# A fused adaLN transformer block: normalising a batch on two engines, Pool's rows ahead of its routing, and three small units half a step later

## The chip, the cores and the metric

The kernel runs on one core of a Trainium2 chip. The metric is the device time in microseconds of one execution: 648.39 us is the median of three (647.23 to 651.87). The core's engines run side by side, each through its own queue in program order, and wait for one another on semaphores: TensorE (PE in the rows, PEld for its weight loads), VectorE (DVE), ScalarE (ACT), GpSimd (POOL), and SyncE (SP), which here only issues DMAs.

## The reference

Eight sequences of 512 tokens with 128 features go through multi-query attention with 16 heads of 8 (one K and V for all heads), then a mixture of experts with 8 experts and top 2, each behind a modulated layer norm.

```python
mod = (_silu(L0_c) @ L0_wmod).reshape(L0_c.shape[0], 6, 1, -1)
h = _layernorm(x) * (1 + ca) + sa
x = x + ga * attention(h)            # softmax(q k^T / sqrt(8)) v, 16 heads, one k and v
h = _layernorm(x) * (1 + cb) + sb
logits = einsum('bth,eh->bte', h, router_w)          # 8 experts, the best 2 taken
h1 = gelu(einsum('bth,efh->btef', h, w1) + b1)
expert_outputs = einsum('btef,ehf->bteh', h1, w2) + b2
x = x + gb * sum(topk_expert_outputs * softmax(topk_values))
```

## The kernel before

**Three stages.** A preparation (to about 65 us) normalises, projects and stores Q, K and V. The attention loop (about 65 to 452 us) does the attention and, beside it, the second layer norm, the router and the routing of the rows. The expert stage (to the end) runs 71 tiles of 128 routed rows.

**The attention loop.** It has 32 groups g: group g does four heads (g mod 4) of batch g // 4. A group has four steps s (128 keys or queries each), a step has four quarter steps j, and two of these are a half step u, for which ScalarE computes one exponential of 128x1024 (L1270). Per half step TensorE issues two quartets of row maxima for the group after next (`maximum(g + 2, s, j)`, L1055), two quartets of scores (`scores`, L1088) and, mostly, two quartets of values (`values`, L1099). VectorE reduces each row-maximum result out of PSUM (L1408). The rows' maxima are turned (L1074), copied by ScalarE (L1295), split in three by GpSimd (L76 to L79) and written by SyncE into the Q operand of the next group, so that the scores come out with the maximum taken off.

**What limits how far TensorE runs ahead.** The maxima and some small units ("maxima turned", "heads turned", "rows turned", "logits", "ranks") share a ring of three PSUM banks: a unit waits until the unit three places before it is reduced by VectorE or copied by ScalarE. `ring_order` lists the units, and TensorE's loop must issue them in the same order. `scores` of a half step waits for the exponential two half steps before it.

**The side work.** For batch b, `batch_at(g, n)` says that group g is 4(b + 1) + n. Counting groups by their number mod 4:

- group 1 mod 4: heads turned (n = 1) and copied by ScalarE (`heads_out`, L1305), ranks of an earlier batch (n = 5; `ranks_out`, L1319); GpSimd does `slots` and `add_attention` (L695 to L699).
- group 2 mod 4: VectorE does four `stats` (L1424) in step 1; GpSimd does `route(b, 0)` and then the variance and a Newton root.
- group 3 mod 4 (n = 3): ScalarE normalises four columns of tokens (`normalize_rows`, L1280), two after the exponential (s, u) = (0, 1), two after (1, 0). GpSimd scales and shifts them (`rows`, L738 to L742). It also does `route` of another batch, pieces 1 and 2. TensorE turns the rows at (s, j) = (3, 3) (L1133).
- group 0 mod 4: logits (n = 4; L1141, copied at L1313); GpSimd does `route(b, 3)` and `top_two`.

`rows` runs in the loop for batches 0 to 5 (groups 7, 11, 15, 19, 23, 27), `route` pieces 1 and 2 in the same place for batches 0 to 4 (groups 11, 15, 19, 23, 27). One `route(b, t)` is two indirect DMAs (L810), each of 128 rows of 576 bytes to places in HBM that the core computed. GpSimd starts them itself. Its order in a group is: split of the next group's maxima, then slots, add_attention, route 0, variance and root, route 1, rows, route 2, route 3, top_two, as far as the group has them.

## Time and profile before

| | us |
|---|---|
| median of the runs | 648.39 |
| the profiled execution | 644.04 |
| its span, first to last instruction | 642.2 |
| PE busy | 568.3 |
| DVE busy | 500.9 |
| ACT busy | 446.0 |
| POOL busy | 318.3 |

The profiled execution is 0.7% under the median. Busy time is a union over the engine's instructions, and for matmuls the ends are modelled, so a busy PE is not a PE without stalls. In rows of a timeline the start of an instruction is what to trust. In the attention loop TensorE shows the same repeating pattern of quartets, so its stalls are read from the distance of two starts.

### The profile page before, as it was taken

To read this page: it belongs to the slowest core of one execution; us is meant where nothing else is said; L and a number is where in the kernel's file an instruction comes from. 1 tells how busy PE (TensorE), PEld (TensorE's weight loads), DVE (VectorE), ACT (ScalarE), POOL (GpSimd) and SP (SyncE) were. 2 spreads that over 40 slices of the span, in tenths; PEclk is the share of its full clock that TensorE was granted. 3 is DMA by queue.
4 is the path that set the end of the run, shared out by engine and by line. 5 is a ranking of instruction groups with operands and counts; after the bars stand their busy time and mean duration, and the time that the engine had idled before them with its cause. 6 is when DMAs were issued, how large, how long until landed. Compare 5 with 4: busy or idle time off the path is not lost.

```text
span 642.2 us, 21095 instructions
## 1 busy us (share of the span) xinstructions
PE 568.3 (88%) x7723; PEld 345.8 (54%) x7723; DVE 500.9 (78%) x1134; ACT 446.0 (69%) x776; POOL 318.3 (50%) x574
## 2 busy tenths in 40 slices
PE   3779999999999999999999999989888897898980
PEld 2222444454544554554454554543777887798970
DVE  5778999898888888888888888786656475555697
ACT  5683688788878878879778878778634452447671
POOL 2633110143476666666566666653166446454571
PEclk9889999999999999999999999999999898799995
DMA  6298300300300310310310310001232122232645
GB/s 182 75 304 301 109 12 8 89 20 8 96 20 26 102 24 26 98 28 22 100 26 26 91 36 24 26 25 30 61 94 67 50 73 85 64 90 59 195 138 169
DMA packets 49877, 49.46 MB, mean 77 GB/s; under 512 B 15616, under 2 KB 44336, under 8 KB 49056
## 3 DMA queue, kind: packets, MB, share of 16 engines
q1 hardware_dynamic: 42256, 36.89, 20.4%
q0 software_dynamic: 4320, 9.38, 4.5%
q10 hardware_dynamic: 3200, 1.84, 1.0%
q8 instruction: 64, 1.05, 0.7%
q14 instruction: 37, 0.30, 0.2%
HBM read 29.40 MB, written 17.10 MB: 72 GB/s over the span
## 4 chain that ended last, share of the span: by engine, by line
PE 66%; DVE 8%; ACT 6%; issue 5%; SPq 4%; another core or an unknown queue 3%; DMA 3%; POOL 1%; DVEq 0%; POOLq 0%; ACTq 0%
PE ps L1055 15%; PE ps L1088 14%; PE ps L1099 13%; PE ps L1178 8%; PE ps L1167 8%; DVE neg_max L1408 3%; ACT P L1270 2%; SPq L956 2%; DMA Q<-max_parts 2%; PE ps L1126 1%; PE ps L1141 1%; SPq L946 1%; PE ps L1158 1%; PE ps L1074 1%
## 5 line engine op out<-in xcount | busy, mean ns | idle before, releaser
L1408 DVE TENSOR_REDUCE neg_max<-ps 128x1 f32<-128x512 f32 x512 | 325.2, 685 | 52.6 <-PE ps L1055 49.6
L1270 ACT ACTIVATE P<-ps,zero 128x1024 f32<-128x1024 f32 x256 | 279.4, 1117 | 71.8 <-PE ps L1088 67.7
L1055 PE MATMUL ps<-K,Q 128*32 128x512 bf16 x2048 | 194.2, 383 | 6.1 <-DVE neg_max L1408 5.0
L1088 PE MATMUL ps<-Q,K 128*32 128x512 bf16 x2048 | 157.1, 381 | 10.7 <-ACT P L1270 4.3
L1099 PE MATMUL ps<-P,V 128*32 128x256 f32 x2048 | 157.7, 382 | 0.5 <-ACT P L1270 0.5
L1620 POOL DMA_INDIRECT y_rows<-P,to_now x71 | 71.3, 1004 | 87.1 <-DVE P L1460 47.5
L1326 ACT ACTIVATE parts<-ps,parts 128x128 f32<-128x128 f32 x228 | 63.8, 382 | 59.1 <-PE ps L1167 27.0
L1055 PEld LDWEIGHTS ps<-K,Q 128*32 128x32 bf16 x2048 | 54.7, 96 | 77.6 <-DVE neg_max L1408 32.0
L1088 PEld LDWEIGHTS ps<-Q,K 128*32 128x32 bf16 x2048 | 52.7, 97 | 69.5 <-ACT P L1270 14.1
L1099 PEld LDWEIGHTS ps<-P,V 128*32 128x32 f32 x2048 | 61.6, 110 | 48.3 <-issue 2.9
L810 POOL DMA_INDIRECT h_sorted<-diag,slot x64 | 64.3, 1004 | 28.6 <-POOL max_parts L79 13.4
L1167 PE MATMUL ps<-parts 128*128 128x128 f32 x456 | 64.8, 282 | 8.6 <-issue 5.8
L1178 PE MATMUL ps<-W,parts 128*128 x456 | 63.1, 283 | 2.6 <-ACT parts L1326 1.5
L1167 PEld LDWEIGHTS ps<-parts 128*128 128x128 f32 x456 | 57.5, 195 | 11.6 <-issue 9.5
L1178 PEld LDWEIGHTS ps<-W,parts 128*128 128x128 f32 x456 | 57.6, 198 | 3.9 <-issue 3.8
L76 POOL CAST max_parts<-neg_max_T 16x128 bf16<-16x128 f32 x32 | 9.0, 281 | 100.0 <-ACT neg_max_T L1295 100.0
L1441 DVE COPY parts<-W 128x644 f32 x57 | 29.8, 523 | 19.3 <-issue 10.3
L1460 DVE TENSOR_TENSOR P<-ps,parts 128x128 f32<-128x128 f32 x57 | 16.3, 285 | 26.7 <-PE ps L1178 14.0
L1326 ACT ACTIVATE P<-ps,P 128x128 f32<-128x128 f32 x56 | 16.0, 371 | 17.2 <-remote 6.7
L1158 PE MATMUL ps<-consts,xs 128*128 128x128 f32 x71 | 19.7, 282 | 0.2 <-issue 0.2
L1448 DVE COPY parts<-ps 128x128 f32<-128x128 f32 x57 | 16.2, 284 | 3.6 <-PE ps L1158 2.8
L1262 ACT COPY att_u<-ps 128x512 f32<-128x512 f32 x32 | 18.5, 577 | 0.8 <-PE ps L1099 0.8
(239 smaller groups left out, 584.3 us busy)
## 6 DMA issues: line engine op xcount, KB each, us to landing
Q<-q_parts SPq DMA_DIRECT2D x24, 384.0 KB
xs<-h_sorted SPq DMA_DIRECT2D x71, 72.0 KB
W<-w_t SPq DMA_DIRECT2D x2, 2048.0 KB, 11.1
q_parts<-parts SPq DMA_DIRECT2D x8, 384.0 KB, 4.0
Q<-y_rows SPq DMA_DIRECT2D x6, 512.0 KB
diag<-att_u SPq DMA_DIRECT2D x128, 16.0 KB
Q<-max_parts SPq DMA_DIRECT2D x96, 4.0 KB
out<-Q SPq DMA_DIRECT2D x6, 256.0 KB, 2.3
```

The lines of the kernel that those rows point to most:

```text
L810: eng.indirect_dma_start(h_sorted, bass.IndirectOffsetOnAxis(ap=slot[p][:, k, t:t + 1], axis=0), hs[p][:, t, :], None).then_inc(routed[p], 16)
L1055: ins = eng.matmul(ring_bank(*unit)[QUAD * q:QUAD * (q + 1), :], Q[buffer_of(g)][:, g % NG * G + j, at:at + QUAD], K[buffer_of(g)][:, 0, : ...
L1088: ins = eng.matmul(to, K[p][:, 1, at:at + QUAD], Q[p][:, first:first + 2, some], start=True, stop=True, tile_position=(0, QUAD * q))
L1099: ins = eng.matmul(bank(7)[QUAD * j:QUAD * (j + 1), some], V[buffer_of(g)][:, s, :], P[s % 2][:, j, some], start=(s == 0 and u == 0), stop ...
L1158: eng.transpose(bank(TURN_BANK[t % 2])[:, 0:TS], xs[t % XD][:, 0:D], ident).then_inc(xsT_done, 1)
L1167: ins = eng.matmul(bank(t % UD)[:, TS * c:TS * (c + 1)], w1_now[t % HD][:, 128 * c:128 * (c + 1)], xsT[t % HD], start=True, stop=True)
L1178: ins = eng.matmul(bank(DOWN_BANK[t % 2])[:, 0:D], hid[t % HD][:, c, :], W2[:, bass.ds(e, 1), c, :].rearrange("p a d -> p (a d)"), start=( ...
L1270: nc.scalar.activation(P[s % 2][:, :, HALF * u:HALF * (u + 1)], bank(2 * u, 2).rearrange("p (j t) -> p j t", j=G), ACT.Exp, bias=zero[:], ...
L1326: nc.scalar.activation(hid[t % HD][:, c, :], bank(t % UD)[:, TS * c:TS * (c + 1)], ACT.Gelu, bias=w1_now[t % HD][:, F + c:F + c + 1]).then ...
L1408: eng.tensor_reduce(neg_max[g % 2][:, j * T + s:j * T + s + 1], ring_bank("maximum", g, s, j), AX.X, ALU.max, negate=True).then_inc(ring_u ...
L1441: eng.tensor_copy(w1_now[t % HD], W1[:, bass.ds(e, 1), :].rearrange("p a d -> p (a d)")).then_inc(w_copied, 1)
L1620: eng.indirect_dma_start(y_rows, bass.IndirectOffsetOnAxis(ap=to_now[t % YD], axis=0), ys[t % YD], None).then_inc(scattered[t % YD], 16)
```

## The change

Four things change.

1. ScalarE normalises only columns 0 and 2 of the batch: column 0 after the exponential (0, 1), column 2 after (1, 1).
2. VectorE normalises columns 1 and 3, each as one `tensor_scalar`: column 1 after the reduction of quarter step (0, 3), column 3 after that of (1, 3). `normalized`, which did this for one late batch only, now takes a list of columns.
3. In GpSimd's queue, `rows` stands ahead of `route(…, 1)`, no longer behind it.
4. Heads, logits and ranks are issued by TensorE at quarter step (2, 1) instead of (1, 3), and copied by ScalarE ahead of the exponential (2, 1) instead of (2, 0). The ring's order follows.

```diff
-                        if s == 1 and j == 3 and batch_at(g, 1) is not None:
+                        if s == 2 and j == 1 and batch_at(g, 1) is not None:
                             units.append(("heads turned", batch_at(g, 1)))
...
-                        if s == 1 and j == 3 and batch_at(g, 4) is not None:
+                        if s == 2 and j == 1 and batch_at(g, 4) is not None:
                             units.append(("logits", batch_at(g, 4)))
-                        if s == 1 and j == 3 and batch_at(g, 5) is not None:
+                        if s == 2 and j == 1 and batch_at(g, 5) is not None:
                             units.append(("ranks", batch_at(g, 5)))
...
-                            if s == 2 and u == 0 and batch_at(g, 1) is not None:
+                            if s == 2 and u == 1 and batch_at(g, 1) is not None:
                                 heads_out(batch_at(g, 1))
...
-                            if s == 0 and u == 1 and batch_at(g, 3) in IN_LOOP:
-                                normalize_rows(batch_at(g, 3), (0, 1))
-                            if s == 1 and u == 0 and batch_at(g, 3) in IN_LOOP:
-                                normalize_rows(batch_at(g, 3), (2, 3))
+                            if s < 2 and u == 1 and batch_at(g, 3) in IN_LOOP:
+                                normalize_row(batch_at(g, 3), 2 * s)
...
-                def normalized(b):
+                def normalized(b, these=range(T)):
...
-                    for n in range(b * T, (b + 1) * T):
+                    for n in (b * T + t for t in these):
                         eng.tensor_scalar(xn2[b % 2][:, n - b * T, :], X[:, n, :], rstd2[:, n:n + 1], shift2[:, n:n + 1],
                                           ALU.mult, ALU.add).then_inc(xn2_done, 1)
...
+                            if s < 2 and j == 3 and batch_at(g, 3) in IN_LOOP:
+                                normalized(batch_at(g, 3), (2 * s + 1,))
...
+                    if batch_at(g, 3) in IN_LOOP:
+                        rows(eng, batch_at(g, 3))
                     if batch_at(g, 7) in EARLY:
                         route(eng, batch_at(g, 7), 1)
-                    if batch_at(g, 3) in IN_LOOP:
-                        rows(eng, batch_at(g, 3))
                     if batch_at(g, 7) in EARLY:
                         route(eng, batch_at(g, 7), 2)
```

GpSimd's queue in a group 3 mod 4 (from group 11 on), before. L79 ends the split of the maxima, each L810 is one indirect DMA of a route, L738 to L742 are `rows`, and L76 begins the split of the next group.

```order
L79 TENSOR_TENSOR max_parts<-max_rest,max_parts 16x128
L810 DMA h_sorted<-diag,slot 34816x144 x2
L738 COPY diag<-consts 128x4
L740 TENSOR_TENSOR diag<-diag,mod_row 128x512
L742 TENSOR_TENSOR diag<-diag,mod_row 128x4x128
L810 DMA h_sorted<-diag,slot 34816x144 x2
L76 CAST max_parts<-neg_max_T 16x128
```

The same place of the changed kernel:

```order
L79 TENSOR_TENSOR max_parts<-max_rest,max_parts 16x128
L738 COPY diag<-consts 128x4
L740 TENSOR_TENSOR diag<-diag,mod_row 128x512
L742 TENSOR_TENSOR diag<-diag,mod_row 128x4x128
L810 DMA h_sorted<-diag,slot 34816x144 x4
L76 CAST max_parts<-neg_max_T 16x128
```

The two pairs of indirect DMAs, which had the two long instructions of `rows` between them, stand together as four in a row.

ScalarE's queue in the same group, before: L1262 copies the finished values of the group before out of PSUM, L1270 is an exponential, L1280 a normalised column, L1309 the copy of the turned rows.

```order
L1295 COPY neg_max_T<-ps 16x128
L1270 ACTIVATE P<-ps,zero 128x4x256
L1262 COPY att_u<-ps 128x512
L1280 ACTIVATE diag<-X,shift,rstd 128x128 x2
L1270 ACTIVATE P<-ps,zero 128x4x256
L1280 ACTIVATE diag<-X,shift,rstd 128x128 x2
L1270 ACTIVATE P<-ps,zero 128x4x256 x5
L1309 COPY diag<-ps 128x512
```

And of the changed kernel (its lines are one to four lower from here on; L1279 is the normalisation):

```order
L1294 COPY neg_max_T<-ps 16x128
L1270 ACTIVATE P<-ps,zero 128x4x256
L1262 COPY att_u<-ps 128x512
L1279 ACTIVATE diag<-X,shift,rstd 128x128
L1270 ACTIVATE P<-ps,zero 128x4x256 x2
L1279 ACTIVATE diag<-X,shift,rstd 128x128
L1270 ACTIVATE P<-ps,zero 128x4x256 x4
L1308 COPY diag<-ps 128x512
```

Two of four columns are gone from ScalarE, and two exponentials stand between the two that are left.

## Rows read from the trace of the kernel before

**Rows 1.** The page: span, and busy time of each engine with its share.

```profile
span 642.2 us, 21095 instructions
...
PE 568.3 (88%) x7723; PEld 345.8 (54%) x7723; DVE 500.9 (78%) x1134; ACT 446.0 (69%) x776; POOL 318.3 (50%) x574
```

**Rows 2.** Windows: us; busy PE, PEld, DVE, ACT, POOL; PE clock; DMA share, GB/s.

```profile
184.00:232.00 48.00, 46.77 (x787) 23.19 (x783) 40.31 (x68) 38.88 (x49) 30.73 (x66) 1.00 0.19 51
...
432.60:435.80 3.20, 3.20 (x32) 1.32 (x36) 2.86 (x10) 2.45 (x3) 1.73 (x5) 0.52 0.03 6
```

**Rows 3.** Groups by shape: count, busy us, mean ns of one, idle before.

```profile
L1408 DVE TENSOR_REDUCE neg_max<-ps 128x1 f32<-128x512 f32 x512 | 325.2, 685 | 52.6 <-PE ps L1055 49.6 <-PE ps L1133 1.4
...
L1431 DVE TENSOR_SCALAR diag<-X,rstd,shift 128x128 f32<-128x128 f32 x8 | 2.2, 342 | 1.9 <-POOL shift L729 1.9
```

**Rows 4.** Timeline of ACT, groups 7 and 8: start, us, instruction, idle before.

```profile
149.67 0.58 ACT L1262 COPY att_u<-ps 128x512 f32<-128x512 f32 x1
150.14 0.89 ACT L1280 ACTIVATE diag<-X,shift,rstd 128x128 f32<-128x128 f32 x2
150.92 1.11 ACT L1270 ACTIVATE P<-ps,zero 128x1024 f32<-128x1024 f32 x1
...
161.81 0.58 ACT L1262 COPY att_u<-ps 128x512 f32<-128x512 f32 x1
```

**Rows 5.** Timeline of PE, group 7; x4 is one quartet, x8 two.

```profile
151.18 0.60 PE L1099 MATMUL ps<-P,V 128*32 128x256 f32 x8
151.61 0.39 PE L1055 MATMUL ps<-K,Q 128*32 128x512 bf16 x4
152.08 0.62 PE L1088 MATMUL ps<-Q,K 128*32 128x512 bf16 x8
...
153.17 0.39 PE L1055 MATMUL ps<-K,Q 128*32 128x512 bf16 x4
153.84 0.40 PE L1088 MATMUL ps<-Q,K 128*32 128x512 bf16 x4 [0.28 <-ACT P L1270]
```

**Rows 6.** Timeline of ACT, groups 15 and 16: the same copy in both.

```profile
246.55 0.58 ACT L1262 COPY att_u<-ps 128x512 f32<-128x512 f32 x1
...
259.36 0.58 ACT L1262 COPY att_u<-ps 128x512 f32<-128x512 f32 x1
```

**Rows 7.** Timeline of POOL, group 15.

```profile
248.09 1.09 POOL L810 DMA_INDIRECT h_sorted<-diag,slot  x1 [0.83 <-POOL max_parts L79]
...
252.09 1.29 POOL L742 TENSOR_TENSOR diag<-diag,mod_row 128x512 f32<-128x512 f32 x1
253.67 1.03 POOL L810 DMA_INDIRECT h_sorted<-diag,slot  x1 [0.28 <-POOL diag L742]
255.00 0.97 POOL L810 DMA_INDIRECT h_sorted<-diag,slot  x1 [0.30 <-issue]
```

**Rows 8.** Timeline of DVE, group 15: the longest wait for a maximum.

```profile
250.42 0.69 DVE L1408 TENSOR_REDUCE neg_max<-ps 128x1 f32<-128x512 f32 x1 [1.44 <-PE ps L1055]
```

**Rows 9.** Timeline of POOL, groups 29 and 30: first and last of four starts.

```profile
425.53 1.08 POOL L810 DMA_INDIRECT h_sorted<-diag,slot  x1 [0.81 <-POOL slot L803]
...
429.44 1.02 POOL L810 DMA_INDIRECT h_sorted<-diag,slot  x1 [0.30 <-issue]
```

**Rows 10.** Timeline of PE, group 30: the scores and the waits before them.

```profile
426.45 0.61 PE L1088 MATMUL ps<-Q,K 128*32 128x512 bf16 x8
...
427.81 0.62 PE L1088 MATMUL ps<-Q,K 128*32 128x512 bf16 x8
...
430.30 0.61 PE L1088 MATMUL ps<-Q,K 128*32 128x512 bf16 x8 [1.39 <-ACT P L1270]
432.60 1.04 PE L1088 MATMUL ps<-Q,K 128*32 128x512 bf16 x8 [1.69 <-ACT P L1270]
```

**Rows 11.** Timeline of ACT, group 30: the exponentials of those two scores.

```profile
429.13 1.11 ACT L1270 ACTIVATE P<-ps,zero 128x1024 f32<-128x1024 f32 x1 [1.82 <-PE ps L1088]
...
431.44 1.10 ACT L1270 ACTIVATE P<-ps,zero 128x1024 f32<-128x1024 f32 x1
```

**Rows 12.** Timeline of POOL and DVE: end of group 13, first stats of 14.

```profile
232.03 1.28 POOL L699 TENSOR_TENSOR X<-X,gated 128x512 f32<-128x512 f32 x1
...
235.13 0.28 DVE L1424 BATCH_NORM_STATS2 ln_stats<-X 128x6 f32<-128x128 f32 x1
```

More of the change, by code:

```diff
@@ L1201, in _ @@
                                 scores(g, s, j // 2)
-                            if s == 1 and j == 3 and batch_at(g, 1) is not None:
+                            if s == 2 and j == 1 and batch_at(g, 1) is not None:
                                 turn_heads(batch_at(g, 1))
@@ L1209, in _ @@
                                 logits(LAST - 1)
-                            if s == 1 and j == 3 and batch_at(g, 4) is not None:
+                            if s == 2 and j == 1 and batch_at(g, 4) is not None:
                                 logits(batch_at(g, 4))
-                            if s == 1 and j == 3 and batch_at(g, 5) is not None:
+                            if s == 2 and j == 1 and batch_at(g, 5) is not None:
                                 ranks(batch_at(g, 5))
@@ L1271, in exponentials, with normalize_row @@
                                          ACT.Exp, bias=zero[:], scale=SCALE).then_inc(exp_done, 1)
-                def normalize_rows(b, tokens):
+                def normalize_row(b, t):
                     eng.wait_ge(rstd2_own, START + (b + 1) * NEWTON_OPS)
@@ L1277, in normalize_rows @@
                         eng.wait_ge(rows_own, START + (b - 1) * ROWS_OPS)
-                    for t in tokens:
-                        n = b * T + t
-                        nc.scalar.activation(xn2[b % 2][:, t, :], X[:, n, :], ACT.Identity, bias=shift2[:, n:n + 1],
-                                             scale=rstd2[:, n:n + 1]).then_inc(xn2_done, 1)
+                    n = b * T + t
+                    nc.scalar.activation(xn2[b % 2][:, t, :], X[:, n, :], ACT.Identity, bias=shift2[:, n:n + 1],
+                                         scale=rstd2[:, n:n + 1]).then_inc(xn2_done, 1)
                 def copy_sums(b, turned):
@@ L1352, in _ @@
                                 turned(batch_at(g, 4))
-                            if s == 2 and u == 0 and batch_at(g, 4) is not None:
+                            if s == 2 and u == 1 and batch_at(g, 4) is not None:
                                 logits_out(batch_at(g, 4))
-                            if s == 2 and u == 0 and batch_at(g, 5) is not None:
+                            if s == 2 and u == 1 and batch_at(g, 5) is not None:
                                 ranks_out(batch_at(g, 5))
@@ L1424, in stats @@
                     eng.bn_stats(ln_stats[:, b * T + t, :], X[:, b * T + t, :]).then_inc(stat_own, 1)
-                def normalized(b):
+                def normalized(b, these=range(T)):
                     eng.wait_ge(rstd2_own, START + (b + 1) * NEWTON_OPS)
-                    eng.wait_ge(rows_own, START + (b - 1) * ROWS_OPS)
-                    for n in range(b * T, (b + 1) * T):
+                    if b >= 2:
+                        eng.wait_ge(rows_own, START + (b - 1) * ROWS_OPS)
+                    for n in (b * T + t for t in these):
                         eng.tensor_scalar(xn2[b % 2][:, n - b * T, :], X[:, n, :], rstd2[:, n:n + 1], shift2[:, n:n + 1],
```

## The prediction

> **What bounds the kernel now.** I read the page first, then windows over the attention loop, then the timelines of PE, ACT, DVE and POOL side by side in the groups that the change touches. The page has TensorE busy for 568.3 of 642.2 us [rows 1]; over four groups of the loop it is 46.77 of 48.00 us, at full clock [rows 2]. TensorE's time is what a change must shorten or lengthen here. Busy is modelled, so I count stalls by starts: two quartets take 151.61 - 151.18 = 0.43 us [rows 5], one 0.215, and whatever two starts lie further apart than that is lost. VectorE is close behind: a reduction is written down with 685 ns [rows 3] and TensorE needs about 0.65 us per maximum.
>
> Group 7 is the one with the normalisation but without routing. From its copy L1262 to the next group's it takes 161.81 - 149.67 = 12.14 us [rows 4]. TensorE loses there 152.08 - 151.61 - 0.215 = 0.25 and 153.84 - 153.17 - 0.215 = 0.45 us, both before scores, the second with ScalarE's exponential as the releaser [rows 5]. So the group would be 11.44 us without stalls. Group 15, with routing, takes 259.36 - 246.55 = 12.81 [rows 6]: 1.37 us of stalls, 0.70 of them like those of group 7 and 0.67 more.
>
> What those 0.67 us are is the centre of this prediction. GpSimd starts an indirect DMA at 248.09 and three more by 255.00 [rows 7]. VectorE, with nothing else to do, gets a maximum from TensorE only at 250.42, after 1.44 us of idleness [rows 8]. The finer case is in groups 29 and 30, the only place where four starts stand together, 425.53 to 429.44 + 1.02 = 430.46 [rows 9]. Scores begun at 426.45 on TensorE reach ScalarE at 429.13, 2.68 us later; those begun at 427.81 at 431.44, 3.63 us later and 0.98 us after the last start's end [rows 10, 11]. Two quartets need 0.43 us of that. So while GpSimd is inside an indirect DMA, word of TensorE's finished work arrives late. I don't know why; the trace shows that it is so. TensorE itself runs on until it needs an answer, and then stands: 430.30 - 427.81 - 0.86 = 1.63 us (two quartets of scores, two of values lie between), and 432.60 - 430.30 - 0.43 = 1.87 us [rows 10], 3.5 us in all.
>
> **The change part by part.**
>
> *ScalarE's two columns less.* Two columns are 0.78 us from start to start (150.92 - 150.14) [rows 4]. Before, ScalarE had an extra 0.47 + 0.78 + 0.78 = 2.03 us within two exponentials (150.14 - 149.67 is the 0.47). An exponential starts every 1.02 us when ScalarE is behind and TensorE asks for one every 1.29 (six quartets), a slack of 0.27. Afterwards it is 0.47 + 0.39 after (0, 1), nothing after (1, 0), 0.39 after (1, 1); by my count of the starts every exponential ends before the scores that need it. I take the whole 0.70 us: **6 groups x 0.70 = -4.2 us**. The least it can be is nothing, if what is left still delays.
>
> *VectorE's two columns more.* 342 ns recorded each [rows 3], about 0.26 in its queue. Twice per group, three and a half quarter steps apart at least, against a ring that lets VectorE be about 0.8 us late before TensorE notices. I take 0. If the cover were gone it would be 6 x 2 x 0.26 = 3.1 us. Here a rule of the Trainium skill bears (SBUF — State Buffer, Who interferes with whom): a `tensor_scalar` may use the port pair that VectorE shares with GpSimd, and whoever comes second is blocked for the other's whole instruction. By it the first column could wait for one of GpSimd's short splits, and the sum would be up to 2 us higher. No row here shows the normalisation beside a busy GpSimd. The second column cannot meet `rows`, which waits for it.
>
> *Rows ahead of routes.* `rows` now starts when the last column is there. In group 11's or 15's times that is about 1 us after `rows` began before; the two long instructions take 1.3 us each (252.09 + 1.29 is the end of the second) [rows 7], so `rows` is done earlier than before and TensorE's turning at (3, 3) does not wait. What is late next are the routes: all four starts come behind, in one run of 1.33 + 3 x 1.27 = 5 us (429.44 + 1.02 - 425.53 = 4.93) [rows 9]. They begin about one step before the group's end and cover the beginning of the next group, where the first exponential, the copy of the turned maxima and VectorE's reductions all wait for TensorE.
>
> The cost of one run of four is bounded from both sides. Below: it costs what the pairs cost now, 0.67 us, so nothing more. Above: the 3.5 us of group 30. I walk it through: counted from the first start, the scores of the next group's first half step begin at about +2.2. Judging by group 30 they are seen at +5.7 to +5.9 (431.44 - 425.53), the exponential ends at +6.9, and only then can TensorE issue the scores two half steps on, due at +4.5: 2.4 us lost, and half a microsecond more because the copy of the turned maxima, which frees a ring bank, stands behind that exponential. I take **2.9 us**, nearer to group 30 because the mechanism is the same and only the work around differs (here the turned rows give TensorE 0.7 us that need no answer, there the maxima are at their end). Against 0.67 now that is +2.2 us for each of the five groups 11, 15, 19, 23, 27: **+11.2 us**.
>
> *Heads, logits, ranks half a step later.* The same work in the same ring distances. In group 1 mod 4 TensorE has no stall to give back; I take 0. GpSimd's work behind the ranks comes about 1.3 us later: `add_attention` ended at 232.03 + 1.28 = 233.31, now at about 234.6. VectorE's first of four stats waits for it; it stood at 235.13, so 0.5 us of slack are left [rows 12]. If that is gone, six groups pay up to 0.8 us each, 5 us. In group 0 mod 4 the later logits may save some tenths of a stall: 0 to -1 us in all, taken as 0.
>
> **The sum.** -4.2 + 11.2 = +7.0 us. On the profiled execution that is 644.04 + 7.0 = 651; the median stands 4.35 us above that execution, so I say 648.39 + 7.0 = 655.4, rounded 655.5.
>
> **The rivals.**
>
> *A. Four starts cost no more than two pairs.* Then ScalarE's gain stands alone: 648.39 - 4.2 = 644.2, with the logits' share 643. This is the case on the other side. It decides at a cost per run of four of 0.67 + 4.2/5 = 1.5 us: below that the kernel is not slower. For it speaks that a pair costs only 0.67; against it that late news does not add up evenly: the first microsecond and a half fall into TensorE's slack and only the rest is lost, so a run twice as long costs more than twice as much. A rule of the Trainium skill is on this rival's side (SBUF — State Buffer, SBUF: two separate sides): PE and ACT never wait on anyone at SBUF's ports, and a DMA cannot be slowed by compute nor slow it. By it four starts would cost TensorE nothing by position. The late results of group 30 don't contradict a rule on ports, but they show that something else is late. Chance 0.3.
>
> *B. The clock falls too.* After the two waits of group 30 the granted clock was 0.52 over the next 3.20 us [rows 2]: TensorE did the work of 1.6 us in that time, a loss of 1.5. If the stall in all five groups is followed by this, add 7.5 us: 663. For it: the waits are alike. Against: between my two waits TensorE does more work than there. Chance 0.15.
>
> *C. The stats wait.* `add_attention` is late for the stats by more than its slack: up to 5 us on top, 660. Chance 0.05.
>
> The forecast itself, a run of four costing 1.5 to 3.7 us, has 0.5 and by itself gives 648.4 to 659.
>
> **How the numbers follow.** The range reaches from A's time, 644, to 664 where B and the upper bound end. Since cases of both signs hold most of the chance, the forecast's own range is 650 to 659. A measurement of this kernel can tell about 1%, 6.5 us, from no change. Faster by over 1% needs 641.9 or less, more than all of ScalarE's gain: 0.05. Slower by over 1% is 654.9 or more: B, C and about half of the forecast's case: 0.47. Within 1%: A and the lower half of the forecast, 0.48.
>
> **What would show each step.** Group 7, which has no routing, should shrink from 12.14 to about 11.45 us between its copies L1262, with no start of scores late; if it doesn't, the first term is wrong. Groups 11 to 27 (every fourth) should grow from 12.8 to about 14.4 us, part of it seen in the group behind, with four starts of L810 about 1.3 us apart, an exponential at the next group's head that waits 2 us or more for PE L1088, and PE starts over 1 us late just behind. If these groups get shorter, A is right. A clock below 1.00 behind these places shows B. The first stats of a group 2 mod 4 with GpSimd as releaser shows C. The groups 1 mod 4 should stay at their time. Most likely to be wrong is the size of a run of four, since one place in the trace has to speak for five.

## The result, and the profile after

| | before | after |
|---|---|---|
| median of 20 executions | 648.94 us (645.02 to 651.96) | 655.89 us (649.9 to 663.81) |
| ratio after / before | | 1.0083, 95% interval 1.0062 to 1.0104 |
| the profiled execution | 644.04 us | 656.22 us |

The changed kernel is 0.8% slower. Three of the 20 executions of after (661.47, 663.81 and 661.15 us) are in a slow state, and the ratio leaves them out while the medians count them. The ratio stands for 5.4 us (4.0 to 6.7), the two medians lie 6.95 us apart, and the two profiled executions 12.2 us. The last of these overstates the change: the profile of before is an execution quicker than all 20 timed ones, that of after an ordinary one. Sums over the two traces are read with that in mind; single places are not touched by it.

The page of after. It answers [rows 1] and, with the reduction L1405, [rows 3] (685 ns, 52.6 us idle):

```profile
span 654.3 us, 21103 instructions
...
PE 568.0 (87%) x7723; PEld 348.5 (53%) x7723; DVE 505.7 (77%) x1146; ACT 442.1 (68%) x764; POOL 318.1 (49%) x574
...
L1405 DVE TENSOR_REDUCE neg_max<-ps 128x1 f32<-128x512 f32 x512 | 328.3, 686 | 58.3 <-PE ps L1055 47.8
...
L1055 PE MATMUL ps<-K,Q 128*32 128x512 bf16 x2048 | 197.0, 386 | 19.2 <-DVE neg_max L1405 17.1
```

TensorE's work is unchanged (568.3 and 568.0 us), ScalarE has 4 us less and VectorE 5 us more. What grew is TensorE's idle time, above all before maxima that wait for VectorE: 19.2 us, where the page of before has 6.1.

**Where it went.** As in the prediction, a group is measured from its copy L1262 to the next one. The groups whose length changed by more than 0.15 us behind the first one:

| groups | before | after | change |
|---|---|---|---|
| 7 (columns, no routing) | 12.14 | 11.41 | -0.73 |
| 11 + 12 | 25.39 | 28.75 | +3.36 |
| 15 + 16 | 25.11 | 26.58 | +1.47 |
| 19 + 20 | 25.79 | 27.24 | +1.45 |
| 23 + 24 | 24.96 | 27.99 | +3.03 |
| 27 + 28 | 25.29 | 26.99 | +1.70 |
| 10, 14, 18, 22, 26 together | 58.89 | 60.38 | +1.49 |
| 25 | 11.77 | 12.30 | +0.53 |
| 29 + 30 + 31 | 33.99 | 34.77 | +0.78 |

The attention loop, from the first copy to the last, went from 371.67 to 384.84 us, +13.2; the expert stage behind it takes the same (189.96 and 189.56).

**A run of four starts, in after.** GpSimd in group 11 (timeline: start, us, instruction, idle before):

```profile
202.89 1.10 POOL L810 DMA_INDIRECT h_sorted<-diag,slot  x1 [0.29 <-POOL diag L742]
204.29 0.97 POOL L810 DMA_INDIRECT h_sorted<-diag,slot  x1 [0.30 <-issue]
205.56 0.96 POOL L810 DMA_INDIRECT h_sorted<-diag,slot  x1 [0.30 <-issue]
206.83 0.95 POOL L810 DMA_INDIRECT h_sorted<-diag,slot  x1 [0.30 <-issue]
```

TensorE, ScalarE and VectorE over it (`remote` means that the profile names no engine of this core as what ended the wait):

```profile
204.27 0.40 PE L1055 MATMUL ps<-K,Q 128*32 128x512 bf16 x4
204.48 0.61 PE L1088 MATMUL ps<-Q,K 128*32 128x512 bf16 x8
204.91 0.40 PE L1055 MATMUL ps<-K,Q 128*32 128x512 bf16 x4
...
205.68 0.28 PE L1074 MATMUL ps<-consts,neg_max 128*16 128x128 f32 x1
206.50 0.40 PE L1055 MATMUL ps<-K,Q 128*32 128x512 bf16 x4 [0.54 <-DVE neg_max L1405]
206.72 0.60 PE L1088 MATMUL ps<-Q,K 128*32 128x512 bf16 x8
209.45 0.62 PE L1055 MATMUL ps<-K,Q 128*32 128x512 bf16 x4 [2.12 <-DVE neg_max L1405]
209.85 1.07 PE L1099 MATMUL ps<-P,V 128*32 128x256 f32 x8
```
```profile
207.31 1.11 ACT L1270 ACTIVATE P<-ps,zero 128x1024 f32<-128x1024 f32 x1 [2.53 <-remote]
208.83 0.26 ACT L1294 COPY neg_max_T<-ps 16x128 f32<-16x128 f32 x1 [0.40 <-remote]
```
```profile
205.75 0.69 DVE L1405 TENSOR_REDUCE neg_max<-ps 128x1 f32<-128x512 f32 x1 [1.71 <-PE ps L1055]
208.70 2.11 DVE L1405 TENSOR_REDUCE neg_max<-ps 128x1 f32<-128x512 f32 x3 [2.26 <-remote]
```

Scores begun at 204.48 reach ScalarE at 207.31, 2.83 us later, much as in [rows 10, 11]. The maximum begun at 204.27 reaches VectorE at 205.75, 1.48 us later, and the one begun at 204.91 only at 208.70, 3.79 us later and behind the last start (206.83 + 0.95 = 207.78). These two free the ring banks that TensorE needs next: the maxima of 206.50 and 209.45 each start 0.06 us after the end of the reduction of the unit three places before (205.75 + 0.69 = 206.44, and the first of the three from 208.70 on, 209.39). TensorE stands 206.50 - 205.68 - 0.21 = 0.61 and 209.45 - 206.72 - 0.43 = 2.30 us: **2.9 us together**. Both waits end with VectorE's reduction. The exponential from 207.31 on was over at 208.42, about 1 us before TensorE went on. The rows can't tell whether the matmuls end late or only the word of it is late, since their ends are modelled.

The other four runs of four in groups 15 to 27 look the same: 0.5 to 0.6 us of standing, then 2.3 us in three of them and 1.6 us in the fourth (group 23). A sixth run of four, from 438.59 to 443.09 + 0.96 = 444.05 in groups 29 and 30, costs far less: group 30 lasts 11.04 us, against 10.63 us where no result is late (run e5 below).

**The clock behind it.** Windows of 3 us behind the five runs of four (columns as in [rows 2]):

```profile
209.80:212.80 3.00, 3.00 (x36) 1.19 (x32) 1.69 (x4) 1.43 (x3) 1.84 (x4) 0.52 0.19 44
262.50:265.50 3.00, 3.00 (x64) 1.53 (x60) 2.99 (x6) 2.70 (x4) 1.84 (x4) 1.00 0.18 49
313.00:316.00 3.00, 3.00 (x60) 1.54 (x56) 2.99 (x6) 2.70 (x4) 1.84 (x4) 1.00 0.20 44
363.40:366.40 3.00, 3.00 (x36) 1.20 (x32) 1.89 (x4) 2.13 (x3) 1.39 (x4) 0.52 0.16 30
416.30:419.30 3.00, 3.00 (x64) 1.53 (x60) 2.99 (x6) 2.70 (x4) 1.84 (x4) 1.00 0.05 11
```

Behind two of five the granted clock was about half, 1.2 instead of 2.4 GHz, and TensorE issued 36 instead of 60 to 64 instructions. These are the groups that lost 3.36 and 3.03 us; the other three lost 1.5 to 1.7.

**The late stretch.** Before TensorE turns the last rows (L1133) there is a wait that before did not have; it ends with VectorE's L742:

```profile
451.28 0.61 PE L1088 MATMUL ps<-Q,K 128*32 128x512 bf16 x8
454.67 0.80 PE L1133 MATMUL ps<-consts,diag 128*128 128x128 f32 x4 [2.77 <-DVE diag L742]
```

### The profile page after: what moved, and what is told of

The parts are those of the page before. It is cut to its first block, busy times and chain, and to the rows that moved or that the text cites. A ratio compares the mean times of both kernels' runs of the same rounds, so it can differ in the third digit from the quotient of the medians.

```text
span 654.3 us, 21103 instructions
## 1 busy us (share of the span) xinstructions
PE 568.0 (87%) x7723; PEld 348.5 (53%) x7723; DVE 505.7 (77%) x1146; ACT 442.1 (68%) x764; POOL 318.1 (49%) x574
## 4 chain that ended last, share of the span: by engine, by line
PE 63%; DVE 8%; SPq 6%; DMA 5%; another core or an unknown queue 5%; issue 4%; POOL 3%; ACT 3%; DVEq 0%; POOLq 0%; ACTq 0%
PE ps L1055 16%; PE ps L1088 13%; PE ps L1099 13%; PE ps L1167 7%; PE ps L1178 7%; DVE neg_max L1405 3%; SPq L956 3%; DMA Q<-max_parts 3%; DMA k_parts<-parts 1%; PE ps L1126 1%; SPq L946 1%; PE ps L1141 1%; POOL h_sorted L810 1%; ACT parts L1325 1%
## 5 line engine op out<-in xcount | busy, mean ns | idle before, releaser
L1405 DVE TENSOR_REDUCE neg_max<-ps 128x1 f32<-128x512 f32 x512 | 328.3, 686 | 58.3 <-PE ps L1055 47.8
L1270 ACT ACTIVATE P<-ps,zero 128x1024 f32<-128x1024 f32 x256 | 279.9, 1116 | 86.6 <-PE ps L1088 64.4
L1055 PE MATMUL ps<-K,Q 128*32 128x512 bf16 x2048 | 197.0, 386 | 19.2 <-DVE neg_max L1405 17.1
L1088 PEld LDWEIGHTS ps<-Q,K 128*32 128x32 bf16 x2048 | 54.2, 97 | 63.2 <-DMA Q<-max_parts 8.7
L810 POOL DMA_INDIRECT h_sorted<-diag,slot x64 | 64.7, 1010 | 26.0 <-issue 13.7
L1167 PE MATMUL ps<-parts 128*128 128x128 f32 x456 | 64.7, 284 | 7.9 <-issue 4.5
L1167 PEld LDWEIGHTS ps<-parts 128*128 128x128 f32 x456 | 58.1, 198 | 10.1 <-issue 7.6
L76 POOL CAST max_parts<-neg_max_T 16x128 bf16<-16x128 f32 x32 | 8.9, 280 | 84.0 <-ACT neg_max_T L1294 82.4
L1262 ACT COPY att_u<-ps 128x512 f32<-128x512 f32 x32 | 18.5, 579 | 2.3 <-PE ps L1099 2.2
```

The lines of the kernel that those rows point to most:

```text
L810: eng.indirect_dma_start(h_sorted, bass.IndirectOffsetOnAxis(ap=slot[p][:, k, t:t + 1], axis=0), hs[p][:, t, :], None).then_inc(routed[p], 16)
L1055: ins = eng.matmul(ring_bank(*unit)[QUAD * q:QUAD * (q + 1), :], Q[buffer_of(g)][:, g % NG * G + j, at:at + QUAD], K[buffer_of(g)][:, 0, : ...
L1088: ins = eng.matmul(to, K[p][:, 1, at:at + QUAD], Q[p][:, first:first + 2, some], start=True, stop=True, tile_position=(0, QUAD * q))
L1167: ins = eng.matmul(bank(t % UD)[:, TS * c:TS * (c + 1)], w1_now[t % HD][:, 128 * c:128 * (c + 1)], xsT[t % HD], start=True, stop=True)
L1270: nc.scalar.activation(P[s % 2][:, :, HALF * u:HALF * (u + 1)], bank(2 * u, 2).rearrange("p (j t) -> p j t", j=G), ACT.Exp, bias=zero[:], ...
L1405: eng.tensor_reduce(neg_max[g % 2][:, j * T + s:j * T + s + 1], ring_bank("maximum", g, s, j), AX.X, ALU.max, negate=True).then_inc(ring_u ...
```

## The experiments

**One fact ahead of all of them.** None of the runs below met the conditions of the first two traces. The chip of those has no number in the results. I call it the first chip, and that it is another one than the four below is inferred from its times. The unchanged kernel before, run beside them, takes 613.8, 614.3, 615.1 and 614.7 us on four other chips (10, 15, 13 and 14 in the tables), where it took 648.9 in the result above. So each ratio below is against before on its own chip.

| run | chip | median us | ratio to before there, 95% interval |
|---|---|---|---|
| e1 after, GpSimd's old order | 10 | 612.85 | 0.9982 (0.9950 to 1.0014) |
| e2 before, GpSimd's new order | 10 | 612.47 | 0.9983 (0.9951 to 1.0014) |
| e3 before, the units later | 10 | 617.39 | 1.0039 (1.0013 to 1.0066) |
| e4 before, the columns shared | 10 | 607.66 | 0.9870 (0.9831 to 0.9910) |
| e5 after, unchanged | 15 | 610.31 | 0.9941 (0.9917 to 0.9964) |
| e6 as e4 | 15 | 607.57 | 0.9914 (0.9882 to 0.9946) |
| e7 as e4, the starts spread | 15 | 611.13 | 0.9966 (0.9934 to 0.9998) |
| e8 as e4, new late stretch | 13 | 607.65 | 0.9885 (0.9839 to 0.9930) |
| e9 after, new late stretch | 13 | 608.09 | 0.9879 (0.9830 to 0.9928) |
| e10 as e2 | 13 | 614.92 | 1.0008 (0.9985 to 1.0032) |
| e11 as e1 | 13 | 614.24 | 0.9984 (0.9953 to 1.0015) |
| e12 as e2 | 14 | 614.03 | 1.0008 (0.9970 to 1.0045) |

### The parts of the change, one by one

The whole change without its third part:

```diff
-                    if batch_at(g, 3) in IN_LOOP:
-                        rows(eng, batch_at(g, 3))
                     if batch_at(g, 7) in EARLY:
                         route(eng, batch_at(g, 7), 1)
+                    if batch_at(g, 3) in IN_LOOP:
+                        rows(eng, batch_at(g, 3))
```

> The changed kernel with one part undone: rows behind the first pair of routes again, so that no four indirect DMA starts stand together in groups 11 to 27. Theory (a run of four starts costs TensorE 2.9 us, two pairs 0.7): about 9 to 14 us less than the changed kernel, the upper end where TensorE's clock fell behind the run of four; against the kernel before -4 us from ScalarE's two columns, +1.5 us for groups 2 mod 4, whose routes come later: 646 to 647 us, ratio 0.995 to 0.998. Groups 11, 15, 19, 23, 27 take about 12.1 us between their copies L1262 and group 7 takes 11.4. Rival (the loss comes from the small units' new place, or from VectorE's columns): stays near the changed kernel's ratio 1.008.

The third part alone, on the kernel before:

```diff
-                    if batch_at(g, 7) in EARLY:
-                        route(eng, batch_at(g, 7), 1)
                     if batch_at(g, 3) in IN_LOOP:
                         rows(eng, batch_at(g, 3))
+                    if batch_at(g, 7) in EARLY:
+                        route(eng, batch_at(g, 7), 1)
```

> The kernel before with only GpSimd's order changed: rows ahead of both pairs of routes. Theory: five runs of four starts at 2.9 us in place of 0.7 us, +11 us, and 1.6 us more for each clock fall behind them: ratio 1.015 to 1.03, slower than the changed kernel. The waits of 0.6 and 2.3 us stand behind each run of four. Rival (the four starts are harmless by position): ratio 1.000.

The fourth part alone (at each of the three units, in the ring's list, in TensorE's loop and in ScalarE's):

```diff
-                            if s == 1 and j == 3 and batch_at(g, 5) is not None:
+                            if s == 2 and j == 1 and batch_at(g, 5) is not None:
                                 ranks(batch_at(g, 5))
```

> The kernel before with only heads, logits and ranks half a step later. Theory: GpSimd's work behind the ranks comes 1.3 us later, its route in groups 2 mod 4 meets VectorE after the four stats: +0.3 us in each of those groups, and the late batch's chain in groups 29 to 31 gets 1 to 3 us longer: +1 to +4 us, ratio 1.002 to 1.006. Rival of the prediction (no effect): 1.000.

The first and second part alone:

```diff
-                                normalize_rows(batch_at(g, 3), (0, 1))
...
-                                normalize_rows(batch_at(g, 3), (2, 3))
+                            if s < 2 and u == 1 and batch_at(g, 3) in IN_LOOP:
+                                normalize_row(batch_at(g, 3), 2 * s)
...
+                            if s < 2 and j == 3 and batch_at(g, 3) in IN_LOOP:
+                                normalized(batch_at(g, 3), (2 * s + 1,))
```

> The kernel before with only the four normalised columns shared by ScalarE and VectorE. Theory: 0.7 us less in each of groups 7, 11, 15, 19, 23, 27, nothing given back: -4.2 us, ratio 0.9935. Rival (the routes' late results fill the stall that ScalarE leaves, so that only group 7 gains): -0.7 us, ratio 0.999. Rival (VectorE blocked at the shared port pair): up to 2 us less gain.

Measured: GpSimd's order alone makes no difference (e2, 0.9983), the units alone cost 0.4% (e3), the columns alone gain 1.3% (e4). The last is more than was forecast: 0.9935 lies outside e4's interval, though inside that of its repetition e6 (0.9914). On this chip my account of the third part fails altogether, and with it the main term of the prediction.

The undo of the third part (e1) came out at 0.9982, and its groups 11, 15, 19, 23 and 27 at 12.76, 12.23, 11.54, 12.05 and 12.25 us, 60.8 together, where 12.1 each was expected. In four of the five TensorE waits 0.6 to 1.3 us for GpSimd's `rows` before it turns them, here in group 15:

```profile
251.68 0.66 PE L1133 MATMUL ps<-consts,diag 128*128 128x128 f32 x4 [0.75 <-POOL diag L742]
```

The same four waits are in e11, the same kernel on another chip (0.5 to 1.25 us, 60.9 us together). They are absent from e4 and e6, which have the units at their old place, and from e5, which has the new order (57.2 us together). So with the units later, GpSimd's chain behind them is later too, and `rows` behind a pair of starts no longer comes in time. The new order takes that away. The third part is worth nothing alone, but about 3.6 us inside the whole change on these chips: 0.9941 (e5) against 0.9982 and 0.9984 (e1, e11). The intervals of these ratios overlap a little; the groups in the traces are what shows it.

### Is it the chip?

The changed kernel itself, nothing edited:

> The changed kernel as it is. The first four experiments ran on a chip on which the kernel before takes 614 us, where TensorE's results are not late beside GpSimd's DMA starts. Theory (the loss hangs on those late results): on a chip where the kernel before takes about 649 us the ratio is 1.008 again and the waits of 0.6 and 2.3 us stand behind each run of four starts; on one where it takes about 614 us they are absent, and the ratio is 0.987 (columns) + 0.004 (units) - 0.002 (order), so 0.99. Rival (the loss belongs to the kernel's order on any chip): 1.008 on either.

Measured: 0.9941, faster than before, where the same code on the first chip gave 1.0083. The two intervals are far apart. Here is e5 at the place shown above, GpSimd, TensorE and ScalarE in group 11:

```profile
202.29 1.10 POOL L810 DMA_INDIRECT h_sorted<-diag,slot  x1 [0.29 <-POOL diag L742]
203.69 0.96 POOL L810 DMA_INDIRECT h_sorted<-diag,slot  x1 [0.30 <-issue]
204.96 0.96 POOL L810 DMA_INDIRECT h_sorted<-diag,slot  x1 [0.30 <-issue]
206.22 0.95 POOL L810 DMA_INDIRECT h_sorted<-diag,slot  x1 [0.30 <-issue]
```
```profile
203.86 0.61 PE L1088 MATMUL ps<-Q,K 128*32 128x512 bf16 x8
...
205.49 0.60 PE L1088 MATMUL ps<-Q,K 128*32 128x512 bf16 x8
205.92 0.39 PE L1055 MATMUL ps<-K,Q 128*32 128x512 bf16 x4
206.14 0.60 PE L1099 MATMUL ps<-P,V 128*32 128x256 f32 x8
206.57 0.39 PE L1055 MATMUL ps<-K,Q 128*32 128x512 bf16 x4
```
```profile
204.58 1.11 ACT L1270 ACTIVATE P<-ps,zero 128x1024 f32<-128x1024 f32 x1 [0.42 <-PE ps L1088]
...
206.21 1.11 ACT L1270 ACTIVATE P<-ps,zero 128x1024 f32<-128x1024 f32 x1 [0.38 <-PE ps L1088]
```

The four starts are as far apart as on the first chip to within 0.01 us, and 1.10 to 0.95 us long as there. But scores begun at 203.86 reach ScalarE at 204.58, 0.72 us later and in the middle of a start, instead of 2.83 us later; and TensorE does not stand. Its group 11 lasts 11.41 us, as group 7 does. So the length of a start is not what differs between the chips. Four starts in a row cost TensorE time in the one trace where its results come late beside them, and none in this one. The rule of the Trainium skill that the prediction put on rival A's side (SBUF — State Buffer, Who interferes with whom: PE and ACT never wait on anyone) agrees with this trace: group 11 lasts 11.41 us beside four starts. On the first chip TensorE loses 2.9 us beside the same starts, though nothing in the rows says that it does so at SBUF.

The same lateness, or its absence, is in the kernel before. Groups 10, 14 and 26, where `route(b, 0)` is two starts and no column is normalised, last 11.8 us in before on the first chip, and 10.7 us on the others (e2, e10, e12). Group 22 is 11.58 against 10.7 to 10.8, while group 18 takes 11.6 to 11.8 on all of them. The first chip also needs 190 us for the expert stage against 167 to 170, at a mean granted clock of 0.92 there against 0.95 in e2 and e5.

The order alone twice more, and the changed kernel with the old order again, each time in the hope of a chip like the first:

> The kernel before with nothing changed but GpSimd's order (rows ahead of the two pairs of indirect DMA starts), on whatever chip it comes to. Theory (the cost of a run of four starts hangs on whether TensorE's results are late beside them, which shows in the kernel before itself as groups 2 mod 4 of 11.8 us rather than 10.7): where the kernel before takes about 649 us, the groups 11, 15, 19, 23, 27 with the one behind each grow by 2.2 us on the 12.8 + 12.5 us, ratio about 1.017, 11 us; where it takes about 614 us, ratio 1.000 +- 0.003 as in the first run of this order. Rival (four starts never cost anything, the changed kernel was longer for another reason): ratio 1.00 on both kinds of chip.

> The changed kernel with GpSimd's old order. Theory: where the kernel before takes about 649 us it loses the 11 us of the runs of four and is left with the columns and the small units: ratio 0.993 to 0.998, against 1.008 of the changed kernel; where it takes about 614 us, 0.998 as before. Rival (the units' later place is what made the changed kernel long there): 1.00 to 1.01 on a 649 us chip.

> GpSimd's order alone on the kernel before, a third time, in the hope of a chip on which the kernel before takes about 649 us. Theory (late results beside the starts are a matter of the chip): there a ratio of about 1.017, with the groups 11 to 27 and the one behind each 2.2 us longer; on a chip where the kernel before takes about 614 us 1.000 +- 0.003. Rival (a run of four starts costs nothing anywhere): 1.00 whatever the kernel before takes.

Measured: before took 615.1 and 614.7 us there, and the ratios are 1.0008, 0.9984 and 1.0008. Three runs of the order alone give no effect within 0.5% on chips 10, 13 and 14. In e10 group 11, which has the new run of four, lasts 12.13 us from copy to copy, as long as its group 7 (162.30 - 150.16 = 12.14) that has no starts at all:

```profile
196.91 0.58 ACT L1262 COPY att_u<-ps 128x512 f32<-128x512 f32 x1
...
209.04 0.58 ACT L1262 COPY att_u<-ps 128x512 f32<-128x512 f32 x1
```

What these runs can't say is what the order alone costs on the first chip. No undo of it was run there, so for that chip the cause is read from its two traces and not shown by an experiment. By e1 and e11 an undo there would also bring back waits for `rows`, so I would expect it to give back less than the 11 us of the expectations (an estimate, from the 3.6 us above).

### The columns, and the starts spread out

The columns alone a second time, and the columns with GpSimd's starts set one by one among its other work:

> The kernel before with only the four normalised columns shared by ScalarE and VectorE, a second time. Theory: -4 us on a 649 us chip, ratio 0.994, with group 7 at 11.4 us and groups 11 to 27 at 12.1; 0.987 to 0.993 on a 614 us chip. Rival (late results take the gain back): group 7 gains 0.7 us and groups 11 to 27 stay at 12.8.

```diff
                     if batch_at(g, 7) in EARLY:
-                        route(eng, batch_at(g, 7), 1)
+                        route(eng, batch_at(g, 7), 1, (0,))
                     if batch_at(g, 3) in IN_LOOP:
-                        rows(eng, batch_at(g, 3))
+                        rows(eng, batch_at(g, 3), (0,))
+                    if batch_at(g, 7) in EARLY:
+                        route(eng, batch_at(g, 7), 1, (1,))
...
+                        rows(eng, batch_at(g, 3), (1,))
```

> The columns alone, and GpSimd's DMA starts of groups 10 to 28 one by one, each with 1.3 us or more of GpSimd's other work (variance, the two instructions of rows, pieces of top_two) or a group's split between it and the next. Theory (one start makes results late by about 1 us, which TensorE's slack of 1.5 us hides; a pair or four in a row do not fit): on a 649 us chip the pairs' losses go, 0.9 us in groups 2 mod 4, 0.7 in 3 mod 4, 0.3 in 0 mod 4: 5 x 1.9 = 9 us less than the columns alone, ratio 0.98. On a 614 us chip nothing to gain, the same as the columns alone. Rival (the loss goes with the number of starts, not with how close they stand): equal to the columns alone on either chip.

Measured: e6 0.9914, e7 0.9966. The two intervals just overlap, and the traces decide: spreading does harm on this chip. A start between the two long halves of `rows` makes the rows late, and TensorE waits to turn them:

```profile
251.29 0.66 PE L1133 MATMUL ps<-consts,diag 128*128 128x128 f32 x4 [0.62 <-POOL diag L742]
```

Its groups 11, 15, 19, 23, 27 last 12.1 us against 11.5 in e6 (12.0 in its group 11). There was nothing to win by it here, since the lateness that it was meant to break up is absent. What spreading would do where results are late wasn't measured.

### The units' cost, and the late stretch

In e3 and e5 the groups 30 and 31 last 10.6 + 13.0 us, in e2 9.28 + 12.59, 1.8 us less. The rest of e3's loop is another 2.1 us longer than e2's, spread over many groups. The largest piece, 0.6 us in group 11, is again a wait for `rows` behind the pair of starts (0.54 us before L1133, ended by GpSimd's L742). Group 14 takes 10.85 to 10.87 us in all five runs with the units later (e1, e3, e5, e9, e11) and 10.68 or 10.69 us in the seven without, so 0.2 us are the units' there. For the rest I have no cause. The chain behind the ranks of batch 5 is long: `slots`, four starts, the split of the last maxima, two starts, the Newton root of batch 6, VectorE's columns and rows, TensorE's L1133. With the ranks half a step later all of it moves. TensorE of e5 in group 30:

```profile
423.44 0.61 PE L1099 MATMUL ps<-P,V 128*32 128x256 f32 x8
426.23 0.62 PE L1088 MATMUL ps<-Q,K 128*32 128x512 bf16 x8 [2.18 <-DMA Q<-max_parts]
...
428.12 0.61 PE L1088 MATMUL ps<-Q,K 128*32 128x512 bf16 x8
431.92 0.90 PE L1133 MATMUL ps<-consts,diag 128*128 128x128 f32 x4 [3.18 <-DVE diag L742]
```

Less the 0.43 us of two quartets, TensorE stands 2.36 us for the last maxima, whose split stands behind the four starts, and 3.37 us for the rows. In e6 they are 1.0 and 3.0 us. To test it, the Newton root was put ahead of the last pieces of routing, the second piece behind the split, and VectorE's last three operations of the first tile list behind the rows; on the columns alone (e8) and on the whole change (e9):

```diff
                     if batch_at(g, 5) == CHUNK[0] - 1:
                         route(eng, CHUNK[0] - 1, 0)
-                        route(eng, CHUNK[0] - 1, 1)
...
                     if batch_at(g, 6) == CHUNK[0] - 1:
-                        route(eng, CHUNK[0] - 1, 2)
+                        route(eng, CHUNK[0] - 1, 1)
                         newton_root(eng, LAST - 1)
+                        route(eng, CHUNK[0] - 1, 2)
                         route(eng, CHUNK[0] - 1, 3)
```

> The shared columns alone, and in the late stretch the Newton root of batch 6 ahead of GpSimd's last two pieces of routing, the second piece behind the split of the last maxima, and the last three operations of VectorE's first list behind the turned batch's rows. If TensorE's wait of 3.0 us before it turns the rows of batch 6 (L1133) is GpSimd's chain, the turning starts about 2.9 us earlier and the 0.8 us wait for the last maxima goes too: 3 to 4 us less than the shared columns alone, a ratio of about 0.986 where those alone had 0.987 to 0.991. Rival (the expert stage's start waits for the lists or the routed rows, not for the attention loop's end): the waits in the loop go and the time stays at 0.99.

> The whole change, with the same new late stretch. If the cost of the later heads, logits and ranks (0.4% as an edit alone) lies in the late chain ranks, slots, starts, root, rows, most of it is hidden now: within 0.2% of the columns with the new late stretch, on a 614 us chip; its waits of 3.3 and 2.4 us before L1133 and L1088 fall below 1.5 us together. Rival (the units cost in every group): it stays 0.3 to 0.5% above the columns with the new late stretch. On a 649 us chip the runs of four add their 11 us either way.

Measured: e9 0.9879 and e8 0.9885. With this late stretch the whole change and the columns alone take the same, 608.09 and 607.65 us, but each interval is about 0.45% to either side, so the times by themselves don't exclude the 0.4% of e3. The traces are clearer. In e9 the groups 30 and 31 last 8.50 + 10.68 us, 19.2 together, instead of e5's 23.6. The wait for the last maxima is gone, and L1133 waits 2.65 us:

```profile
426.77 0.61 PE L1091 MATMUL ps<-Q,K 128*32 128x512 bf16 x8
429.85 0.66 PE L1136 MATMUL ps<-consts,diag 128*128 128x128 f32 x4 [2.46 <-DVE diag L742]
```

Of the 4.5 us, 1.6 come back as a longer wait at the head of the expert stage (L1170, three lines later than L1167):

```profile
442.00 1.90 PE L1170 MATMUL ps<-parts 128*128 128x128 f32 x8 [3.35 <-DVE parts L1449]
```

against 1.71 us in e5. For the columns alone the expectation of 3 to 4 us was wrong: L1133 waits 2.0 instead of 3.0 us, the clock behind it was 0.55 over 3.5 us in e8's execution and 1.00 in e6's, and groups 30 and 31 together are as long as in e6 (20.21 and 20.27 us). The Newton root ran only from 423.24 on, since the split waits for the last maxima (L1297) until 417.82 and the two starts for it. So no version was found that beats the columns alone by more than the intervals: e4, e6 and e8 at 0.987 to 0.991, 607.6 us all three. Against the changed kernel on chip 15 (610.31) that is 2.7 us. On the first chip it wasn't tried.

## Why the prediction was right, and where it was wrong

**The time** was forecast as 655.5 us, within 644 to 664; 655.89 was measured. That the two are 0.4 us apart is in part luck, as the terms show. On the first chip's two traces:

*ScalarE's two columns less, -0.70 us a group.* Right: group 7 went from 12.14 to 11.41 us, and no start of scores in it is late. It holds on the others too: 12.13 to 12.15 in e2, e3, e10, e12, and 11.40 or 11.41 in e4, e5, e6.

*VectorE's columns, nothing.* Right, in that the gain came whole in group 7. The two engines do meet, at a small price that TensorE doesn't see. In group 7 of after the first column runs on VectorE from 148.83 to 149.17, and GpSimd's split has to wait for 0.47 us before its next instruction, where it waits 0.17 in groups 11 to 27:

```profile
148.83 0.34 DVE L1429 TENSOR_SCALAR diag<-X,rstd,shift 128x128 f32<-128x128 f32 x1
```
```profile
149.20 0.28 POOL L78 CAST max_parts<-max_rest 16x128 bf16<-16x128 f32 x1 [0.47 <-POOL max_rest L77]
```

In groups 15, 19 and 23 it is VectorE's column that takes 0.44 instead of 0.33 us beside the same instruction. That fits the rule of the Trainium skill that the prediction named (SBUF — State Buffer, Who interferes with whom: the two share a port pair, and the second to come is blocked). Here it costs 0.1 to 0.3 us a meeting, on an engine that TensorE does not wait for.

*A run of four costs 2.9 us.* Right on the first chip in size and in its first cause, the late results: 0.61 + 2.30 us at the place walked through, about 2.9 us in four of the five runs and 2.2 us in the fifth. The net change of three of the pairs of groups is +1.5 to +1.7, where -0.7 + 2.2 = +1.5 was expected. But the path was another one, and that the size fits owes something to luck. The prediction had the scores of the next group's first half step seen by ScalarE at +5.7 to +5.9 us from the first start, and TensorE held by the exponential behind them for 2.4 us and by the copy of the turned maxima for half a microsecond. They were seen at +4.4 (207.31 - 202.89), and both waits were for ring banks that VectorE freed late. The sixth run of four, in groups 29 and 30 of after, shows how much the price hangs on the place. On four other chips the same four starts cost nothing, and the forecast would have been wrong in sign: 0.9941 is rival A's case to within its interval (4.2 us of 614 is 0.993). What the prediction read out of one place in the trace belonged to where the program ran, not to the program alone.

*The units later, nothing.* Wrong in size, by 0.4% (e3, 1.0039). Of the 3.9 us that e3's loop is longer than e2's, 1.8 are the late chain. The step looked at group 1 mod 4 and at the stats of the in-loop batches. They are as forecast: groups 13, 17 and 21 keep their 11.77 us, the stats do not wait (rival C). But the ranks of the last routed batch in the loop have a longer chain behind them than any other, to L1133 of batch 6, and this was not followed. Nor was it followed that `rows` hangs on the same chain in groups 11 to 27, which the new order hides (e1, e11). In the first chip's traces the loss at the end is masked: groups 29 to 31 grew by 0.78 us only, because the four starts there (438.59 in after, 425.53 in [rows 9]) moved to a place where less waits for them, and group 29 lost its wait (14.20 to 11.12 us).

*Rival B, the clock.* Put at a chance of 0.15 and at all five places, it came true at two of five, with about the 1.5 us each that was worked out: 3.36 and 3.03 against 1.5 to 1.7. It is the largest part by which the profiled difference passes the sum.

*The sum.* Predicted +7.0 us on the profiled execution, found +12.2: +3.5 more in the groups 11 to 28 (the clock's two falls are about 3 of it), +1.5 in the groups 2 mod 4, +0.5 in group 25, +0.8 at the end, and 1.1 less outside the loop (0.7 before its first copy, 0.4 in the expert stage). The first of these is explained. The 0.5 us of group 25 are the units': e5 has them too (12.28 us), with the same wait of 0.33 us for the maxima (`DMA Q<-max_parts`) as after (0.35). Of the groups 2 mod 4 the units explain 0.2 us in group 14, the rest is not tested. So terms of about +5 us are missing from the sum. The medians don't show it, because the profiled execution of before was a quick one, 4.9 us under the median of 20, while that of after was ordinary. Two traces of one execution each can't settle a sum to better than that.

**What stays open:** why TensorE's results come late beside GpSimd's indirect starts on one chip and not on four others, whether it belongs to the chip or to something that ran beside it, which of GpSimd's starts and the transfers that they set off does it, and what the order alone costs where they do.

## What to carry to other kernels

Before a wait that nothing in the program explains is made the main term of a sum, ask whether it is the program's or the machine's: run the unchanged kernel on another chip and look at the same place. Parts of a change are not terms that add up: GpSimd's new order was worth nothing alone and 3.6 us beside the later units. When a step is moved later, follow its longest chain of followers, which is that of the last batch, not the typical one. Sharing a load between two engines at places where both have slack gave its full, forecast gain in group 7 on every chip; moving DMA starts together was free on four and cost 2.2 to 2.9 us a run on one.

## What the runs showed of the hardware

- One program takes 649 us on one chip and 614 to 615 us on four others, about 5.6% apart, with instructions of nearly the same length: a reduction is recorded with 685 and 686 ns, an indirect start with 0.95 to 1.10 us on both. Of the difference between the traces of before and e2, 10 us are in the attention loop and 21 us in the expert stage, where the mean granted clock is 0.92 against 0.95.
- On the first chip scores reach ScalarE 2.83 us and a maximum reaches VectorE 3.79 us after their starts beside four indirect DMA starts, the latter only behind the last of them. In e5 the scores take 0.72 us at the same place.
- A `tensor_scalar` of 128x128 on VectorE and a small instruction of GpSimd's split delay each other by 0.1 to 0.3 us when they meet (group 7: GpSimd's wait 0.47 instead of 0.17 us; groups 15, 19, 23: the column 0.44 instead of 0.33 us).
- Behind a stand of 2.3 us (0.6 us before it) the granted clock fell to 0.52 over 3 us in one case out of four, and behind the one of 1.6 us it fell too; the length of the last wait alone does not decide it.
